# Two inputs loaded ahead of the large weights, and a third stage with four batches in quarters of the array

## The reference

```
q = einsum('bcn,dc->bnd', x, Wq) + bq          # 16 features
k = einsum('bcn,dc->bdn', ctx, Wk) + bk
v = einsum('bcn,dc->bdn', ctx, Wv) + bv
x = einsum('bcm,bnm->bcn', v, softmax(q @ k, axis=2)) + x
g, theta, phi = conv1x1(g_w, ctx), conv1x1(theta_w, x), conv1x1(phi_w, ctx)   # 64 channels
y = (theta^T phi / 256) g^T
out = gamma * (w_w y + w_b - mean) / sqrt(var + eps) + beta + x
```

## Time and profile before

| | |
|---|---|
| median of 3 runs | 1354.14 us (1354.11 to 1356.47) |
| profiled execution | 1354.62 us, of which the span from first to last instruction is 1352.9 us |
| TensorE busy | 1239.4 us, 92% of the span |
| VectorE, ScalarE, GpSimd busy | 943.3, 841.6, 502.6 us |
| mean granted TensorE clock | 0.976 of full |
| moved by the DMA engines in the first 60 us | 10.7 MB |
| first stage, second stage, third stage | 0 to 476, 476 to 1237, 1237 to 1352.9 us |

### The profile page before, as it was taken

The page is one execution under the profiler, slowest core; times in us unless marked ns, Lnnn a source line. Parts: engine busy times, 40 slices in busy tenths (PEclk is TensorE's granted clock), DMA queues, the critical chain, the costliest instruction groups (busy, mean ns, idle before and its releaser), DMA issues. The chain is left out here.

```text
span 1352.9 us, 31159 instructions
## 1 busy us (share of the span) xinstructions
PE 1239.4 (92%) x10866; PEld 1005.2 (74%) x10866; DVE 943.3 (70%) x1843; ACT 841.6 (62%) x2495; POOL 502.6 (37%) x490
## 2 busy tenths in 40 slices
PE   4688999999998759999999999999999999995997
PEld 3477788788776658888888888888888888882554
DVE  3688988988977366676766666667666666662554
ACT  3488988888886365555555665656556556552443
POOL 3355654654534013333333333333333333342000
PEclk8899999999999969999999999999999999997999
DMA  8000000000000020000000000000000000000100
GB/s 317 9 13 21 16 16 12 11 16 13 8 7 1 1 78 2 1 10 1 9 0 0 9 0 0 9 0 8 1 0 9 0 0 1 1 1 26 47 31 31
DMA packets 18547, 24.96 MB, mean 18 GB/s; under 512 B 1360, under 2 KB 16912, under 8 KB 18064
## 3 DMA queue, kind: packets, MB, share of 16 engines
q1 hardware_dynamic: 18448, 23.77, 5.2%
HBM read 21.67 MB, written 2.10 MB: 18 GB/s over the span
## 5 line engine op out<-in xcount | busy, mean ns | idle before, releaser
L1195 POOL TENSOR_TENSOR prob<-prob,l_z_inv 128x512 f32<-128x512 f32 x256 | 261.2, 1042 | 458.6 <-DVE l_z_inv L1436 458.6
L1355 ACT ACTIVATE prob<-psum,l_neg_max 128x256 f32<-128x256 f32 x512 | 236.0, 473 | 247.1 <-DVE l_neg_max L1430 232.6
L742 ACT ACTIVATE ring_e<-ring_e,neg_max 128x128 f32<-128x128 f32 x512 | 164.3, 407 | 21.3 <-DVE neg_max L911 21.2
L1430 DVE TENSOR_REDUCE l_neg_max<-psum 128x2 f32<-128x512 f32 x256 | 163.9, 681 | 10.7 <-PE psum L1249 10.7
L1261 PEld LDWEIGHTS psum<-ident,prob 128*128 128x128 f32 x1024 | 109.8, 141 | 49.0 <-issue 45.4
L1277 PE MATMUL psum<-pT,vs 128*64 128x256 f32 x1024 | 138.8, 391 | 6.7 <-DVE aTl L1446 6.5
L1261 PE MATMUL psum<-ident,prob 128*128 128x128 f32 x1024 | 139.9, 280 | 0.0
L1441 DVE COPY pT<-psum 128x512 f32<-128x512 f32 x128 | 88.1, 688 | 50.6 <-PE psum L1261 50.5
L449 POOL TENSOR_TENSOR ring_e<-ring_e,cross_add 128x512 f32<-128x512 f32 x64 | 85.3, 1350 | 90.8 <-DVE ring_e L906 90.8
L449 POOL TENSOR_TENSOR ring_e<-ring_e,self_add 128x512 f32<-128x512 f32 x64 | 86.0, 1357 | 63.1 <-DVE ring_e L906 62.4
L1446 DVE TENSOR_TENSOR aTl<-psum,aTh 128x256 fp32r<-128x256 f32 x128 | 54.4, 425 | 74.2 <-ACT aTh L1370 74.2
(11 more groups left out here) (198 smaller groups left out, 3200.6 us busy)
## 6 DMA issues: line engine op xcount, KB each, us to landing
wz_raw<-wz_in SPq DMA_DIRECT2D x2, 1536.0 KB, 14.6
x_in<-x SPq DMA_DIRECT2D x8, 256.0 KB, 2.9
cT<-ctxT SPq DMA_DIRECT2D x8, 256.0 KB, 2.8
w<-w_in SPq DMA_DIRECT2D x2, 1024.0 KB, 11.3
l_ub<-ctx_in SPq DMA_DIRECT2D x8, 256.0 KB, 2.7
cg<-ctx_in SPq DMA_DIRECT2D x4, 512.0 KB, 3.7
out<-fin SPq DMA_DIRECT2D x4, 512.0 KB, 2.8
wi_raw<-wi_in SPq DMA_DIRECT2D x1, 1536.0 KB, 18.0
```

The source lines that it names most:

```text
L742: last = nc.scalar.activation(e, e, ACT.Exp, bias=neg_max[:, n % RE, h:h + 1])
L1195: pool.tensor_tensor(e, e, z_inv[:, t % RE, h, :].unsqueeze(2).broadcast_to([P, 2, D]), ALU.mult)\
L1355: last = nc.scalar.activation(prob[:, t % RE, h, qt * D:(qt + 1) * D], score_bank[h][:, qt * D:(qt + 1) * D], ACT.Exp, bias=neg_max[:, t % ...
L1430: nc.vector.tensor_reduce(neg_max[:, t % RE, h, :], score_bank[h].rearrange("p (t c) -> p t c", t=2), AX.X, ALU.max, negate=True).then_inc ...
```

## The change

**Order of the loads.** The second pair's input is issued behind the rows and the self mask, ahead of the first context; the third pair's behind `wkv`, `wao`, `wq` and the first cross mask, ahead of `wco`, `w1`, `w2` and the second stage's weights. Both keep the waits of `next_x`.

**Third stage.** The queries and keys of the four batches are made in four quarters (32 columns) of the array, and the scores in four row quarters, each batch with a PSUM bank of its own, in which the turned probabilities land too. Gram, heads, thetas and last maps put two batches in the halves. Queries and keys have one fill, thetas one. The copy of x and three memsets are gone. GpSimd divides (`norm`) and adds the output's bias to x beforehand (`bias`), so that VectorE makes the output in one pass per half. The rounds are written out and overlap: queries, keys, values and scores of the next round are issued within a round, thetas and last maps of a round within the next. The tiles `cg`, `x2`, `x2b` and `fin` exist twice; contexts 0 and 1 are loaded at the start, context i + 2 behind the store of round i.

```diff
--- before.py
+++ after.py
@@ -377,22 +377,26 @@
                 sp.wait_ge(*cross_add_made.at(i - 1))
                 load_mask(i)
 
+            def load_weights(*named):
+                for w, src, s in named:
+                    sp.dma_start(w[:, :, :], v[src].rearrange("(c p) n -> p c n", p=P)).then_inc(s, 16)
+
             load_x(0)
             sp.dma_start(cols[:, :], v["cols_in"]).then_inc(w_cols, 16)
-            sp.dma_start(wqkv[:, :, :], v["wqkv_in"].rearrange("(c p) n -> p c n", p=P)).then_inc(w_qkv, 16)
+            load_weights((wqkv, "wqkv_in", w_qkv))
+            sp.dma_start(self_mul[:, :], v["smask"]).then_inc(w_mask, 16)
             sp.dma_start(rows[:, :], v["rows_in"].partition_broadcast(P)).then_inc(w_rows, 16)
-            sp.dma_start(self_mul[:, :], v["smask"]).then_inc(w_mask, 16)
+            next_x(1)
             load_ctx(0)
+            load_weights((wkv, "wkv_in", w_kv), (wao, "wao_in", w_ao), (wq, "wq_in", w_q))
             load_mask(0)
-            for w, src, s in ((wkv, "wkv_in", w_kv), (wao, "wao_in", w_ao), (wq, "wq_in", w_q),
-                              (wco, "wco_in", w_co), (w1, "w1_in", w_1), (w2, "w2_in", w_2)):
-                sp.dma_start(w[:, :, :], v[src].rearrange("(c p) n -> p c n", p=P)).then_inc(s, 16)
+            next_x(2)
+            load_weights((wco, "wco_in", w_co), (w1, "w1_in", w_1), (w2, "w2_in", w_2))
             for w, src, c in ((wz0_raw, "wz_in", 0), (wz1_raw, "wz_in", 1), (wi0_raw, "wi_in", 0)):
                 sp.dma_start(w[:, :], v[src][c * P:(c + 1) * P, :]).then_inc(l1_weights_in, 16)
-            for g in range(1, R0 + 2):
-                if g >= 3:
-                    next_ctx(g - 2)
-                    next_mask(g - 2)
+            for g in range(3, R0 + 2):
+                next_ctx(g - 2)
+                next_mask(g - 2)
                 if g < R0:
                     next_x(g)
             sp.wait_ge(w_mask, 16)
@@ -1562,7 +1566,7 @@
     (psum, xs, ident, half_neg, col) = (v[n] for n in ("psum", "xs", "ident", "half_neg", "col"))
     DK = 16
     CI = 64
-    RE, RT = 4, 2
+    QROWS = P // G
...
+        cg = [sb(f"cg{k}", [P, G, D]) for k in range(2)]
+
+
+        qk = sb("l2_qk", [P, 2, D])
...
+        gT = sb("gT", [P, 2, CI])
+        hw = sb("hw", [P, 2, P])
+        theta = sb("theta", [P, 2, D])
+        prob = sb("l2_prob", [P, G, BANK])
+        pT = sb("l2_pT", [P, G, BANK])
+        x2 = [sb(f"x2_{k}", [P, G, D]) for k in range(2)]
+        x2b = [sb(f"x2b_{k}", [P, G, D]) for k in range(2)]
+        fin = [sb(f"fin{k}", [P, G, D]) for k in range(2)]
...
+        score_bank = [psum[:, b, :] for b in range(G)]
+        wide = Banks(ctx, nc, "l2_wide", ["p0", "p1", "p2", "p3", "y0", "y1"], [psum[:, 4 + j, :] for j in range(2)])
+        work = Banks(ctx, nc, "l2_work", ["qk", "w0", "w1", "w2", "w3", "t", "g", "h"],
+                     [psum[:, 6 + j, :] for j in range(2)])
...
+            def load(i):
+                sp.dma_start(cg[i % 2][:, :, :], v["ctx_in"].rearrange("b p d -> p b d")[:, i * G:(i + 1) * G, :])\
+                    .then_inc(ctx_in[i % 2].sem, 16)
+
+            def store(i):
+                sp.wait_ge(*wide.out("y1", i))
+                sp.wait_ge(*wide.out("y0", i))
+                sp.dma_start(v["out"].rearrange("b p d -> p b d")[:, i * G:(i + 1) * G, :], fin[i % 2][:, :, :])\
+                    .then_inc(out_written[i % 2].sem, 16)
+
+            sp.dma_start(wqk[:, :, :], v["wqk2_in"].rearrange("p (t n) -> p t n", t=2)).then_inc(weights_in, 16)
+            load(0)
             sp.dma_start(wvpg[:, :], v["wvpg_in"]).then_inc(weights_in, 16)
...
             sp.dma_start(bvpg[:, :], v["rows_in"][ROWS["bvpg"]:ROWS["bvpg"] + D].partition_broadcast(P))\
                 .then_inc(weights_in, 16)
...
+            sp.dma_start(wtheta[:, :], v["theta_in"]).then_inc(weights_in, 16)
+            for h in range(2):
+                sp.dma_start(ww[h * CI:(h + 1) * CI, :], v["ww_in"]).then_inc(weights_in, 16)
+            load(1)
+            for i in range(ROUNDS):
+                store(i)
+                if i + 2 < ROUNDS:
+                    sp.wait_ge(*work.full("w3", i))
+                    load(i + 2)
+            for i in (ROUNDS - 2, ROUNDS - 1):
+                sp.wait_ge(*out_written[i % 2].at(i // 2))
...
-            pool.memset(q2[:, :, :], 0.0).then_inc(zeroed, 1)
-            pool.memset(k2[:, :, :], 0.0).then_inc(zeroed, 1)
-            pool.memset(gT[:, :, :], 0.0).then_inc(zeroed, 1)
...
+            def norm(i, b):
+                pool.wait_ge(*z_inv_done.at(i, b))
+                e = prob[:, b, :].rearrange("p (t c) -> p t c", t=2)
+                pool.tensor_tensor(e, e, z_inv[:, b, :].unsqueeze(2).broadcast_to([P, 2, D]), ALU.mult)\
+                    .then_inc(probs_done.sem, 1)
+
+            def bias(i, b):
+                pool.wait_ge(*wide.out(f"p{b}", i))
+                if b == 0:
+                    pool.wait_ge(*wide.out("y0", i - 2))
+                    pool.wait_ge(*wide.out("y1", i - 2))
+                pool.tensor_scalar(x2b[i % 2][:, b, :], x2[i % 2][:, b, :], bn[:, 3:4], None, ALU.add)\
+                    .then_inc(x2_biased.sem, 1)
+
+            for i in range(ROUNDS):
+                for b in range(G):
+                    norm(i, b)
+                for b in range(G):
+                    bias(i, b)
...
-            with pe.Fori(0, ROUNDS) as i:
-                pe.wait_ge(*x_copied.at(i))
+            def quarter(b):
+                return slice(b * QROWS, (b + 1) * QROWS)
...
+            def half(b):
+                return slice(b % 2 * CI, (b % 2 + 1) * CI)
...
+            def queries_keys(i):
+                ps = work.psum("qk")
+                pe.wait_ge(*work.free("qk", i))
+                pe.wait_ge(*ctx_in[i % 2].at(i // 2))
+                for t in range(2):
+                    for b in range(G):
+                        src = xs[:, i * G + b, :] if t == 0 else cg[i % 2][:, b, :]
+                        last = mm(ps[quarter(b), t * D:(t + 1) * D], wqk[:, t, :], src, start=True, stop=True)
+                last.then_inc(work.fills("qk"), 1)
...
+            def scores(i):
+                pe.wait_ge(*work.out("qk", i))
+                for b in range(G):
+                    pe.wait_ge(*probsT_done.at(i - 1, b))
+                for qt in range(2):
+                    for b in range(G):
+                        last = mm(score_bank[b][:, qt * D:(qt + 1) * D], qk[quarter(b), 0, qt * P:(qt + 1) * P],
+                                  qk[quarter(b), 1, :], start=True, stop=True)
+                        if qt == 1:
+                            last.then_inc(scores_done.sem, 1)
...
+                    for j in range(2):
+                        for b in (2 * m, 2 * m + 1):
+                            last = mm(ps[half(b), m * CI:(m + 1) * CI], vpg[:, b, j, P + CI:D], vpg[:, b, j, P:P + CI],
+                                      start=j == 0, stop=j == 1)
+                last.then_inc(work.fills("g"), 1)
...
+                    for b in (2 * m, 2 * m + 1):
+                        last = mm(ps[half(b), m * P:(m + 1) * P], gT[half(b), m, :], ww[half(b), :],
...
+            def thetas(i):
+                ps = work.psum("t")
+                pe.wait_ge(*work.free("t", i + 1))
+                pe.wait_ge(*wide.out(f"p{G - 2}", i))
+                pe.wait_ge(*wide.out(f"p{G - 1}", i))
+                for m in range(2):
+                    for b in (2 * m, 2 * m + 1):
+                        last = mm(ps[half(b), m * D:(m + 1) * D], wtheta[:, :], x2[i % 2][:, b, :],
+                                  start=True, stop=True)
+                last.then_inc(work.fills("t"), 1)
...
                     for b in (2 * m, 2 * m + 1):
-                        last = mm(ps[:, b % 2 * D:(b % 2 + 1) * D], hw[:, b, :], theta[:, b, :],
+                        last = mm(wide.psum(f"y{b % 2}")[:, m * D:(m + 1) * D], hw[half(b), m, :], theta[half(b), m, :],
                                   start=True, stop=True)
-                    last.then_inc(work.fills(f"y{m}"), 1)
+                        if m == 1:
+                            last.then_inc(wide.fills(f"y{b % 2}"), 1)
...
+            pe.wait_ge(weights_in, 96)
+            queries_keys(0)
+            for b in range(G):
+                values(0, b)
+            scores(0)
+            for i in range(ROUNDS):
+                more = i + 1 < ROUNDS
+                gram(i)
+                if i > 0:
+                    last_maps(i - 1)
+                turn(i, 0)
+                turn(i, 1)
+                heads(i)
+                times_v(i, 0)
+                turn(i, 2)
+                if more:
+                    queries_keys(i + 1)
+                times_v(i, 1)
+                turn(i, 3)
+                times_v(i, 2)
+                if more:
+                    values(i + 1, 0)
+                times_v(i, 3)
+                if more:
```

(126 more changed lines are left out.)

264 lines of the change are left out of this document (65 added, 199 removed).

## The result

The changed kernel takes 1333.61 us, median of 4 runs (1332.02 to 1336.98), against 1354.64 (1354.11 to 1356.47) for the kernel before in the same comparison: a ratio of 0.9846, 95% interval 0.9824 to 0.9867. I had said 1333, with 1323 to 1342. The profiled execution took 1332.02 us; its span is 1330.3, against 1352.9.

The account below looks back on a forecast made before the run. It took VectorE's input stall at the start and TensorE in program order in the third stage as the bounds. 1354.62 - 8.0 (loads) - 13.4 (third stage) = 1333.2, median 0.5 under, 1332.7: predicted 1333, range 1323 to 1342.

Parts of the forecast that it names:

- The loads: Start of the kernel: second pair's input lands before VectorE asks, the other moved loads cost zero; 8.0 us saved.
- The stall's second price: Start: after TensorE's empty stretch its work runs at the lower clock; four steps take 3.0 us instead of 6.6 without it.
- TensorE's sum: Third stage, one round: TensorE's products priced at 15.8 us plus 0.4 for drains, 16.2 against 23.3.
- The gap before values 3: Third-stage round: TensorE stands from 2.1 to 4.5 us, as values 3 needs the bank of values 1.
- The wait for the context: Third stage, bodies 1 and 2: queries and keys wait for a context load issued behind the store; 3.9 us lost each.
- The clock behind it: After the context's wait TensorE runs one stretch at the lower clock, about 1.7 us a hit (bounds 0 and 2.5).
- Rival 1: Third stage: the clock holds over the 3.9 us wait; 1330 us, or 1329 with a quick load; chance 0.21.
- Rival 2: Third stage: the context's wait is hidden by a later chain or quick load; rounds of 19, 1322 us; chance 0.08.
- rival 4: Start: the reordered loads buy little, gain 0 to 4 us; 1337 to 1341 us; chance 0.09.
- rival 3: Third stage: hand-overs and another clock dip after the gap before values 3 add 5 to 9; 1338 to 1342; chance 0.12.
- Rival 5: Third stage stays at the lower clock, rounds of 35 us; slower, about 1374 us in total; chance 0.03.
- Rival 6: Third stage: packed products don't overlap, 6 us a round back; 1353 us; chance 0.03.

Follow-up runs that it names:

- e6: Changed kernel with each context load ahead of the store, and VectorE's reads of values 1 and 2 ahead of maxima 2 and 3: 1314.18 us.
- e2: Changed kernel with the old order of the loads, so only the third stage is new: 1340.5 us.
- e1: Kernel before with only the new order of the loads, third stage as before: 1346.89 us.
- e7: Changed kernel with the third pair's input behind the big weights again, only the second pair's ahead of them: 1333.39 us.
- e3: Changed kernel with each context load issued ahead of the store of the round before: 1322.43 us.
- e4: Changed kernel with nine products, their results overwritten, ahead of TensorE's wait for the context in two rounds: 1331.28 us.
- e5: Changed kernel with the division of the probabilities back on VectorE, GpSimd keeping the bias adds: 1344.06 us.
- e9: e6 with all four heads products of a round taken from rows 0 to 63, so the output differs: 1313.93 us.
- e8: Changed kernel with only VectorE's reads of values 1 and 2 ahead of maxima 2 and 3, store still ahead of load: 1327.76 us.

## Why the prediction was right, step by step

**The loads.** Right in cause and size. x(1) was in before VectorE asked, and nothing waited for the loads behind it: the first context was used at 48.79, as said. The turn of 38.66, said for 34.1, starts at 32.43 in the changed kernel, since there the values' product before it takes 1.89 us, not the 3.22 of the profile before. That is a matter of the execution and not of the change: in e6's profile, which has the same loads, the product takes 3.23 and the turn starts at 33.99, and both have the sums at nearly the same time, 35.74 and 35.89. The stall's second price varies too: e2 still has the stall, and its turn behind it takes 1.09 as in the earlier trace rows, but its sums take 1.07 and not 1.93. I took 8.0; e1 gives 8.0 between medians. A single profile would not have shown this: the nine profiles with the new order (e7's among them) have the third stage's first weight load between 1227.17 and 1232.39, mean 1230.2, against 1238.63 and 1238.84 (e2) with the old one. Two rows of the changed kernel and of e7, the same product at the same place, show one source of the spread. The first is the changed kernel's timeline, the second e7's:

```profile
84.81 2.09 PE L587 MATMUL psum<-kT,qT 32*128 32x128 f32 x32
```

```profile
84.75 1.17 PE L587 MATMUL psum<-kT,qT 32*128 32x128 f32 x32
```

Before each stands one turn behind a wait of 1.02 and 1.01 us; the clock fell behind it in one execution and not in the other.

**TensorE's sum.** 15.8 plus 0.4, and e6 has 15.18. Gram and heads were sized too high: eight heads records take 0.65, not 1.08, and the gram's 0.69, not 1.0. Together they make 0.7 of the 1.0 by which the sum is off. The other products came close to their prices.

**The gap before values 3.** 2.4 said, 2.21 measured, by VectorE's order as laid out.

**The store.** Said for 12.1 us after values 1, measured at 10.65 (1270.24 - 1259.59): reciprocal 3 ended at 9.3 in place of 10.1. The steps were the right ones, 0.8 us shorter up to that reciprocal and 0.6 behind it.

**The wait for the context.** Right in place and cause, slightly low in size: 4.36 and 4.18 against 3.9. I had let the load land 4.1 us after its start; TensorE went on 4.9 and 4.75 us after its issue, near my upper bound. e3 priced the whole, 11.2 us where I had 11.

**The clock behind it.** 1.7 said; from the queries to the next values 1 the rounds took 7.81 and 7.80 us, the first round, which has no such wait, 6.17 (1253.42 to 1259.59). So 1.6, and e4, with the wait filled, shows 6.17 again. Rival 1 is out. The 1.6 is the low end: the ten such waits of all profiles cost 1.6 to 2.7.

**The rounds.** 24.6 said, 23.82 and 23.64 measured; the first 13.6 said and 14.10 measured; the last 24.4 said, 23.25 measured; from the first load to the end of the first scores 13.7 said, 13.9 measured. The sum is 2.2 us shorter than mine, from the earlier store and the shorter gram and heads. That is the difference between 13.4 and 15.6; the loads' 7.0 of 8.0 in this execution took back 1.0 of it.

The first round holds a cost that the prediction left out. Its turn starts 3.3 us after the scores, as said, but at the lower clock:

```profile
1248.77 2.12 PE L1760 MATMUL psum<-ident,l_prob 128*128 128x128 f32 x8 [2.59 <-POOL l_prob L1679]
1250.82 1.12 PE L1752 MATMUL psum<-ww,gT 64*64 64x128 f32 x8
```

In the later rounds the same two take 1.09 and 0.65; the shorter gram and heads hid part of the difference. All nine profiles that have the new third stage show the lower clock behind this wait, and it lasts for two lengths: the first round takes 14.1 to 14.2 us in three of them (the changed kernel, e2, e4) and 16.0 to 16.1 in six. What decides between them stays open.

**How much of the fit is luck.** Some. The profiled execution came 1.2 us under the 1333.2 that I had added up for it, out of misses of 2.2 and 1.0 that partly cancel. It is also the fastest of its four; the others take up to 5 us more, and the median lies 1.6 us above it, which happens to bring it to the number forecast. The steps are right by their own rows; the total is closer than they are.

**The other rivals.** Rival 2 is out by the waits of 4.36 and 4.18 us, rival 4 by e1. The drops of the clock (rival 3) after the gap of 2.2 us didn't come in the changed kernel's profile, but in those of e3, e4 and e7 they did in five of nine rounds, at 1.2 to 1.6 us each (from values 3 to the turns: 5.2 to 5.7 us there, 4.05 in the changed kernel). What decides it in a given execution stays open. Rival 5, the lower clock through whole rounds, did not come: the windows show 0.93. Rival 6 neither: thetas 1.08, maps 1.13, queries and keys 0.64 and 0.61.

## What to carry to other kernels

When a program's rounds are made to overlap, look again at every load that used to be a round ahead: here one issue standing ahead of another in SP's order cost 11 us, half as much as the whole change brought. Price every long idle bracket of TensorE that is left with the lower clock behind it as well (1.6 to 2.7 us behind each wait for the context here). An engine that frees a bank should do so before work that is needed later: reading the values out earlier gave 5.9 us in the changed kernel and 8.3 with the load ahead of the store, and putting the division on the quicker engine, ahead of that read, lost 10.

## What the runs showed of the hardware

- After a wait of 4.2 to 5.1 us, TensorE fell to the lower clock each time, ten times in five kernels. The first queries behind it could still be at full speed (0.64 in the changed kernel's second wait); times v behind them took 1.95 to 2.08. From the queries to the next values 1 it needed 7.8 to 8.9 us, against 6.17 at full speed, so the price was 1.6 to 2.7 us. It did not follow the length of the wait: 4.65 us cost 1.6 (e2), 4.23 us cost 2.3 (e7). After a wait of 3.4 us the clock fell three times of three (e5), after one of 2.2 us five times of fifteen. With the long wait filled by products it did not fall there (e4), but in that execution it fell behind the next gap of 2.2 us.
- Products in two column halves of the array overlap. The gram's sixteen records, of the same shape, took 1.15 us in one half and 0.69 in two; the heads' eight took 1.16 before and 0.65 after, whether their inputs came from one row half (e9) or from two. The Trainium skill, TensorEngine Tiling (Array Packing), Restrictions and Gotchas, says that different row tiles cannot use the same PSUM bank at the same time. The heads of the changed kernel use two row halves in one bank, in other partitions of it, and e9, in which only one row half is used, takes the same 0.65: no such cost is seen here. A case in which two row tiles write the same partitions was not tried.
- A context load of 0.5 MB right behind a store of 0.5 MB held TensorE until 4.75 to 5.65 us after its issue (the changed kernel and e8). The two such loads of the changed kernel landed in 4.7 us, median; the four of the kernel before, none of them right behind a store, in 3.7.
